# Zero matmuls in TensorE's waits, another order of the first four units, and four rounds of ones on ScalarE, in a one-core DLRM tower

## What is computed

```python
e = stack([tbl_f[ids[:, f]] for f in range(40)], axis=1)    # 512 x 40 x 32, 40 table lookups
i, j = triu_indices(40, k=1)                                # 780 pairs of fields
z = einsum('bpd,pde,bpe->bp', e[:, i], bilinear, e[:, j])   # one 32x32 matrix a pair
h = concatenate([z, dense_ctx], axis=1)                     # 512 x 796
h = maximum(h @ W_top1 + b_top1, 0)                         # 512 wide
h = maximum(h @ W_top2 + b_top2, 0)                         # 256 wide
y = h @ W_top3
```

## Time and profile before

| | us |
|---|---|
| median of 3 runs | 204.15 (202.26 to 205.39) |
| the profiled execution | 202.93 |
| its span, first to last instruction | 201.1 |
| TensorE busy in the span | 180.2 |
| VectorE busy in the span | 159.4 |
| ScalarE busy in the span | 50.9 |

### The profile page before, as it was taken

The page is one execution under the profiler, slowest core; times in us unless marked ns, Lnnn a source line. Parts: engine busy times, 40 slices in busy tenths (PEclk is TensorE's granted clock), DMA queues, the critical chain, the costliest instruction groups (busy, mean ns, idle before and its releaser), DMA issues.

```text
span 201.1 us, 3168 instructions
## 1 busy us (share of the span) xinstructions
PE 180.2 (90%) x1328; PEld 55.9 (28%) x1328; DVE 159.4 (79%) x158; ACT 50.9 (25%) x83; POOL 96.6 (48%) x101
## 2 busy tenths in 40 slices
PE   0097959949999999999999999999999999999992
PEld 0032212302432222322323222223232222223442
DVE  0779995999899999999999874996998989741500
ACT  2001095195000394010025413116204000031520
POOL 3877777887777777777777777400000000000000
PEclk9999988996999999999999999999999999999998
DMA  6999700000000581011001001000000000000000
GB/s 166 384 390 405 284 13 13 13 15 10 16 15 13 171 326 15 13 16 14 13 14 17 16 13 14 10 3 0 0 3 2 0 0 0 3 0 0 0 0 0
DMA packets 7662, 12.07 MB, mean 60 GB/s; under 512 B 2752, under 2 KB 5712, under 8 KB 7520
## 3 DMA queue, kind: packets, MB, share of 16 engines
q1 hardware_dynamic: 4288, 10.24, 13.9%
q0 software_dynamic: 3072, 1.58, 4.7%
q10 hardware_dynamic: 288, 0.05, 0.2%
HBM read 11.86 MB, written 0.00 MB: 59 GB/s over the span
## 4 chain that ended last, share of the span: by engine, by line
PE 80%; DVE 14%; DMA 3%; issue 1%; SPq 0%; ACT 0%; DVEq 0%
PE y_ps L469 30%; PE z_ps L491 24%; PE t_ps L450 10%; PE t_ps L438 8%; DVE hot L363 6%; PE y_ps L505 3%; DMA table<-hot_tables 3%; DVE low L375 3%; DVE rest L373 3%; DVE prod L404 2%; PE y_ps L422 2%; PE y_ps L499 2%; PE t_ps L514 1%; PE z_ps L484 0%; DVE xt L380 0%
## 5 line engine op out<-in xcount | busy, mean ns | idle before, releaser
L404 DVE TENSOR_TENSOR prod<-y_ps,xt 128x1024 f32<-128x1024 f32 x100 | 115.6, 1216 | 17.1 <-PE y_ps L469 9.1
L268 POOL DMA_INDIRECT x_rows<-rows,row x96 | 96.1, 1001 | 29.2 <-issue 28.9
L469 PE MATMUL y_ps<-xt,m_sb 32*128 32x512 f32 x400 | 67.5, 658 | 0.0
L491 PE MATMUL z_ps<-prod,sel 128*32 128x512 f32 x400 | 53.3, 604 | 0.0
L338 ACT ACTIVATE xt<-xt 128x512 f32<-128x512 f32 (+2 forms) x60 | 36.6, 625 | 17.3 <-DVE xt L380 15.9
L469 PEld LDWEIGHTS y_ps<-xt,m_sb 32*128 32x128 f32 x400 | 23.4, 187 | 39.6 <-issue 32.1
L438 PE MATMUL t_ps<-hot,table 128*32 128x512 bf16 x144 | 15.9, 431 | 17.4 <-DVE low L375 16.4
L363 DVE TENSOR_SCALAR hot<-hot_id,number 128x2048 bf16<-128x2048 int16 x36 | 25.7, 760 | 7.1 <-DMA hot_id<-hot_ids 5.8
L450 PE MATMUL t_ps<-z_t,table 128*128 128x512 f32 x40 | 21.4, 634 | 0.0
L491 PEld LDWEIGHTS z_ps<-prod,sel 128*32 128x32 f32 x400 | 7.9, 107 | 38.6 <-issue 31.0
L342 ACT ACTIVATE z_t<-z_ps 128x512 f32<-128x512 f32 x7 | 4.2, 597 | 54.0 <-PE z_ps L491 54.0
(11 more groups left out here) (21 smaller groups left out, 35.8 us busy)
## 6 DMA issues: line engine op xcount, KB each, us to landing
hot_id<-hot_ids SPq DMA_DIRECT2D x4, 512.0 KB, 7.0
table<-w SPq DMA_DIRECT2D x1, 1792.0 KB, 7.6
x_rows<-rows,row POOLq DMA_INDIRECT x96, 2.4
table<-hot_tables SPq DMA_DIRECT2D x2, 640.0 KB, 9.5
table<-hot_tables SPq DMA_DIRECT2D x2, 512.0 KB, 6.4
m_sb<-mats SPq DMA_DIRECT2D x2, 512.0 KB, 12.5
m_sb<-mats SPq DMA_DIRECT2D x2, 384.0 KB, 11.0
m_sb<-mats SPq DMA_DIRECT2D x1, 640.0 KB
```

What stands on the lines that cost most here:

```text
L268: pool.indirect_dma_start(out=x_rows[:, g, c, :], out_offset=None, in_=rows, in_offset=bass.IndirectOffsetOnAxis(ap=row[:, n:n + 1], axis= ...
L404: nc.vector.tensor_tensor(prod[:, k % PROD_UNITS, 2 * half:2 * half + 2, :], y_ps[:, 2 * slot:2 * slot + 2, :], partners[half], ALU.mult). ...
L469: last = nc.tensor.matmul(y_ps[:, 2 * slot + place % 2, :], m_sb[rows, k, :], xt[rows, u, :], start=True, stop=True)
L491: last = nc.tensor.matmul(z_ps[s * DIM:(s + 1) * DIM, :], window, prod[:, k % PROD_UNITS, place, :], start=first, stop=(k == last_unit(b)) ...
```

## The change

`UNIT[0:4]` becomes (2,0), (2,1), (0,0), (1,1). VectorE clears one piece of `prod` as its first instruction, and TensorE then multiplies these zeros 24 times (`WARM`). It also multiplies zeros in front of rounds 8 and 16 (`SPLIT_FILL`, 7 matmuls each), three times four behind unit 0 and once four behind unit 6 (`FILL`). The ones of rounds 5, 9, 14 and 20 (`BY_SCALAR`) are made by ScalarE in two activations, |id - row| and relu(1 - that), into blocks 1 to 6 of `z_t`, which are free then. The ring of four is shared by the 32 rounds that VectorE keeps. `AFTER` has new numbers: 26 rounds stand ahead of all units where 19 did, and 15 mixes where 7 did.

```diff
+UNIT[0:4] = UNIT[2:4] + UNIT[0:2]
+WARM = 24
+FILL = 4
+SPLIT_FILL = 7
+BY_SCALAR = {5: 0, 9: 0, 14: 8, 20: 16}
+ONES_RING = 3
 AFTER = {
-    "hot": [-1, -1, -1, -1, -1, -1, -1, -1, -1, -1, -1, -1, -1, -1, -1, -1, -1, -1, -1, 0, 1, 1, 1, 1, 1, 1, 2, 2, 2,
-        3, 3, 3, 3, 4, 5, 8],
-    "l1": [18, 24, 27, 28, 29, 29, 30, 30, 31, 33, 34, 34, 41, 42, 43, 45, 47, 48, 49, 49],
-    "turn": [0, 8, 18, 24, 32, 33],
-    "mix": [-1, -1, -1, -1, -1, -1, -1, 0, 0, 0, 0, 0, 1, 1, 1, 1, 2, 4, 4, 5, 6, 6, 7, 7, 9, 9, 10, 10, 11, 11, 11,
-        12, 13, 13, 13, 14, 17, 20, 24, 24, 25, 26, 27, 27, 27, 28, 29, 29, 35, 37, 38, 38, 39, 39, 40, 41, 43, 45,
-        49, 50],
+    "fill": [0, 0, 0, 6],
+    "hot": [-1, -1, -1, -1, -1, -1, -1, -1, -1, -1, -1, -1, -1, -1, -1, -1, -1, -1, -1, -1, -1, -1, -1, -1, -1, -1, 0,
+        1, 1, 4, 6, 6, 6, 6, 6, 7],
+    "l1": [18, 24, 26, 27, 28, 28, 31, 32, 33, 34, 36, 37, 41, 41, 43, 44, 46, 47, 48, 49],
+    "turn": [0, 8, 18, 24, 32, 38],
+    "mix": [-1, -1, -1, -1, -1, -1, -1, -1, -1, -1, -1, -1, -1, -1, -1, 0, 0, 1, 2, 2, 3, 3, 3, 5, 7, 7, 7, 9, 9, 11,
+        12, 13, 14, 14, 14, 14, 18, 20, 25, 25, 25, 26, 26, 26, 26, 28, 29, 32, 34, 34, 35, 35, 36, 36, 36, 37, 38,
+        42, 43, 45],
 }
@@ schedule()
-        for what in ("hot", "l1", "mix"):
+        for what in ("fill", "hot", "l1", "mix"):
@@ ones(j), new: where a round's ones lie
+            if j in BY_SCALAR:
+                n = 2 * (scalar_rounds.index(j) % ONES_RING)
+                return z_t[:, 1 + n:3 + n, :]...  # as bf16
+            return hot[:, vector_rounds.index(j) % HOT_RING, :, :]
@@ scalar
             act.dma_start(number[:], numbers).then_inc(number_in, 16)
+            act.dma_start(negative[:], negatives).then_inc(negative_in, 16)
             act.dma_start(sel[:], select).then_inc(sel_in, 16)
             for what, k in steps:
+                if what == "hot":
+                    for j in [j for j in scalar_rounds if BY_SCALAR[j] == k]:
+                        o, r = ROUND[j]
+                        n = scalar_rounds.index(j)
+                        act.wait_ge(hot_id_in[o], 16)
+                        act.wait_ge(negative_in, 16)
+                        if n >= ONES_RING:
+                            act.wait_ge(hot_used, scalar_rounds[n - ONES_RING] + 1)
+                        columns = ones(j).rearrange("p f b -> p (f b)")
+                        nc.scalar.activation(columns, hot_id[:, o, :], ACT.Abs,
+                                             bias=negative[:, n:n + 1]).then_inc(ones_half, 1)
+                        act.wait_ge(ones_half, n + 1)
+                        nc.scalar.activation(columns, columns, ACT.Relu, bias=negative[:, len(BY_SCALAR):],
+                                             scale=-1.0).then_inc(ones_done, 1)
@@ vector
+            nc.vector.memset(prod[:, 0, 0, :], 0.0).then_inc(cleared, 1)
             dve.wait_ge(number_in, 16)
...
-                    if k >= HOT_RING:
-                        dve.wait_ge(hot_used, k - HOT_RING + 1)
-                    nc.vector.tensor_scalar(hot[:, k % HOT_RING, :, :]...
+                    if k not in BY_SCALAR:
+                        n = vector_rounds.index(k)
+                        if n >= HOT_RING:
+                            dve.wait_ge(hot_used, vector_rounds[n - HOT_RING] + 1)
+                        nc.vector.tensor_scalar(ones(k)...
@@ tensor
+            def fill(count, start):
+                for _ in range(count):
+                    nc.tensor.matmul(z_ps[0:DIM, :], sel[:, 0:SEL_COLS].bitcast(BF16)[:, 0:DIM],
+                                     hot_id[:, 1, 0:BATCH].bitcast(BF16), start=start, stop=start,
+                                     skip_group_check=True)
+            pe.wait_ge(cleared, 1)
+            zeros = prod[:, 0, 0, :].bitcast(BF16)
+            for _ in range(WARM):
+                nc.tensor.matmul(y_ps[:, 0, :], zeros[:, BATCH:BATCH + P], zeros[:, 0:BATCH], start=True, stop=True)
             for what, k in steps:
+                if what == "fill":
+                    fill(FILL, AFTER["fill"][k] < LAG)
                 if what == "hot":
+                    if r == 0 and o == 1:
+                        pe.wait_ge(sel_in, 16)
+                        pe.wait_ge(hot_id_in[1], 16)
+                    if r == 0 and o > 0 and AFTER["hot"][k] < 0:
+                        fill(SPLIT_FILL, True)
...
-                    pe.wait_ge(hot_done, k + 1)
+                    if k in BY_SCALAR:
+                        pe.wait_ge(ones_done, scalar_rounds.index(k) + 1)
+                    else:
+                        pe.wait_ge(hot_done, vector_rounds.index(k) + 1)
...
-                    if u == t:
-                        x_there(pe, t)
+                    if all(w != u for _, w in UNIT[:k]):
+                        x_there(pe, u)
```

More of the change, by code:

```diff
@@ L136, in vector_schedule, with ones_count @@
     return steps
+def ones_count(k, by_scalar):
+    return len([j for j in range(k + 1) if (j in BY_SCALAR) == by_scalar])
 def picked(o):
@@ L148, in ends_bank, with bass_dlrm_tower @@
     return what == "hot" and k in [picked(o) for o in range(HOTS)]
-def bass_dlrm_tower(nc, ids, rows, hot_ids, numbers, hot_tables, dense, mats, w1, b1, w2, b2, w3, select, dense_sel, out):
+def bass_dlrm_tower(nc, ids, rows, hot_ids, numbers, negatives, hot_tables, dense, mats, w1, b1, w2, b2, w3, select, dense_sel, out):
     steps = schedule()
@@ L173, in x_there @@
             engine.wait_ge(turned, GATHER_POS.index(t) + 1)
+    vector_rounds = [j for j in range(len(ROUND)) if j not in BY_SCALAR]
+    scalar_rounds = [j for j in range(len(ROUND)) if j in BY_SCALAR]
     def mix_slot(g, s):
@@ L205, in bass_dlrm_tower @@
         number = sb("number", [P, HOTS, MAX_ROWS])
+        negative = sb("negative", [P, len(BY_SCALAR) + 1])
         hot = sb("hot", [P, HOT_RING, G, BATCH], BF16)
@@ L217, in bass_dlrm_tower, with ones @@
         w1_sb = weight_cols[:, 0:BLOCKS * N1].rearrange("p (b n) -> p b n", b=BLOCKS)
+        def ones(j):
+            if j in BY_SCALAR:
+                n = 2 * (scalar_rounds.index(j) % ONES_RING)
+                return z_t[:, 1 + n:3 + n, :].rearrange("p b c -> p (b c)").bitcast(BF16).rearrange(
+                    "p (f c) -> p f c", f=G)
+            return hot[:, vector_rounds.index(j) % HOT_RING, :, :]
         def upper(words):
@@ L226, in bass_dlrm_tower @@
         ids_in = sem("ids_in")
+        cleared = sem("cleared")
+        ones_half = sem("ones_half")
+        ones_done = sem("ones_done")
         row_done = sem("row_done")
         number_in = sem("number_in")
+        negative_in = sem("negative_in")
         hot_id_in = [sem(f"hot_id_in{o}") for o in range(HOTS)]
@@ L360, in _ @@
                         dve.wait_ge(hot_id_in[o], 16)
-                    if k >= HOT_RING:
-                        dve.wait_ge(hot_used, k - HOT_RING + 1)
-                    nc.vector.tensor_scalar(hot[:, k % HOT_RING, :, :].rearrange("p f b -> p (f b)"),
-                                            hot_id[:, o, :], number[:, o, r:r + 1], None,
-                                            ALU.is_equal).then_inc(hot_done, 1)
+                    if k not in BY_SCALAR:
+                        n = vector_rounds.index(k)
+                        if n >= HOT_RING:
+                            dve.wait_ge(hot_used, vector_rounds[n - HOT_RING] + 1)
+                        nc.vector.tensor_scalar(ones(k).rearrange("p f b -> p (f b)"), hot_id[:, o, :],
+                                                number[:, o, r:r + 1], None, ALU.is_equal).then_inc(hot_done, 1)
                     if r == 0:
@@ L387, in _ @@
                     t, u = UNIT[k]
-                    if u == 0 and t >= 2:
+                    if u != t and all(v == w or v != t for v, w in UNIT[:k]):
                         x_there(dve, t)
@@ L438, in _ @@
                             last = nc.tensor.matmul(t_ps[f * DIM:(f + 1) * DIM, :], pieces[piece][:, f, :],
-                                                    hot[:, k % HOT_RING, f, :], start=(r == 0 and piece == 0),
+                                                    ones(k)[:, f, :], start=(r == 0 and piece == 0),
                                                     stop=(r == n - 1 and piece == 2), skip_group_check=True)
@@ L565 @@
         numbers[:, o, :n] = np.arange(P * n).reshape(P, n)
+    negatives = np.ones((P, len(BY_SCALAR) + 1), np.float32)
+    for n, j in enumerate(sorted(BY_SCALAR)):
+        o, r = ROUND[j]
+        negatives[:, n] = -(np.arange(P) * HOT_ROWS[o] + r)
     hot_tables = np.zeros((P, HOTS, G, MAX_ROWS, DIM), np.float32)
@@ L577 @@
         "numbers": numbers,
+        "negatives": negatives,
         "hot_tables": hot_tables.reshape(P, HOTS, G, MAX_ROWS * DIM),
```

## The result

The changed kernel takes 193.74 us (median of 4 runs, 193.54 to 194.19) against 203.2 for the kernel before (201.77 to 205.39). The ratio is 0.956, 95% interval 0.948 to 0.964. The profiled execution of the changed kernel takes 193.84 us; its span is 192.0, 9.1 us less than before.

The account below looks back on a forecast made before the run. VectorE's queue, with 4.5 us idle, was taken to bound the head up to unit 8. Head -6.8 and steps +0.3 gave -6.5 us: 196.4 from 202.93, 197.7 from the median; 197.0 given, range 194.5 to 200.4.

Parts of the forecast that it names:

- the head: From 9.64 us until VectorE starts unit 8 at 65.91; forecast 6.8 us shorter, from 7.3 and 6.5.
- Rivals 2 and 3: Zeros don't count for the clock: 204.3 us, chance 0.06; Abs and Relu each need a table load: 205, 0.04.
- rivals 1 and 4: Clock falls once or twice: 198.7 to 200.4 us, chance 0.12; gain lost behind unit 8: 199, 0.06.
- everything behind it follows at a fixed distance: Behind VectorE's queue up to unit 8: what comes off that road comes off the end.
- small extra DMA: Load of the added input at the start, said to lie in VectorE's wait for the first ids until 5.76 us.
- My walk: VectorE's queue followed step by step from 9.64 us: table 3's pieces end at 34.0, unit 8 at 59.4 by pace.
- Busy time less the four comparisons: VectorE from 9.64 us to unit 8: 51.75 - 2.8 = 48.9 us, so unit 8 at 58.6.
- The first layer's steps: Steps placed between units behind unit 8: +0.4, -0.4, +0.2 and 0 to 0.6 more, taken as +0.3 us.
- the base: Time the gain is taken from: profiled execution 202.93 us gives 196.4, median 204.15 gives 197.7; 197.0 given.
- nine more rounds on VectorE: Walk's rounds after 24.0 us, said to reach 29.6 on VectorE with TensorE at 30.6.
- The first product's 2.4 us: Wait of 2.37 us before unit 0, put down to ScalarE's mixes; said to vanish with (2,0) first.
- the turns stand further ahead of their use: Transposes behind unit 8, with the mixes: ahead of their use by more than the 6.8 us they lose.

Follow-up runs that it names:

- a_noscalar: Changed kernel with all 36 rounds of ones on VectorE, none on ScalarE: 196.64 us.
- a_nowarm: Changed kernel without its 24 first zero matmuls, the 30 later ones kept: 196.01 us.
- b_again: Kernel before, run once more unchanged: 203.03 us, ratio 1.0003.
- b_warm: Kernel before plus the memset, the 24 first zero matmuls and the added input with its load; order and rounds as before: 201.13 us, ratio 0.993.
- t_tensor: Kernel before plus the small 128x5 input alone, loaded by nobody: 201.15 us, ratio 0.9924.
- t variants: Kernel before with small additions alone, such as an input, a load or a memset; usable times 201.2, 201.15 and 203.04 us.
- t_dup: Kernel before plus one more small load on ScalarE's queue from an existing input, no new tensor: 203.04 us, ratio 1.004.
- t_memset: Kernel before plus the memset and TensorE's wait for it; run under the disturbance, time not usable, wait for the output's transfer 2.5 us.
- e_notensor: Changed kernel without the added input, its numbers in free columns of `numbers`; disturbed, time not usable, wait for the output's transfer 2.5 us.
- a_nofill: Changed kernel with its 24 first zero matmuls but without the other 30: 194.03 us.
- a_order_only: Changed kernel without any zero matmul and with all rounds on VectorE; new order and added input stay: 198.82 us.
- b_scalar: Kernel before with rounds 5, 9, 14 and 20 on ScalarE and the added input; order as before, no zeros: 200.86 us, ratio 0.991.

## Why the prediction was right or wrong

**The bound was right.** VectorE's queue sets the head, and what leaves it reaches the end: the two later stages kept their length within 0.1 us. The comparisons cost 0.7 us each (a_noscalar), the 24 zeros hide in the wait for the first table and the first rounds are fast (a_nowarm), the later ones hide too. Rivals 2 and 3 (zeros don't count, ScalarE too slow by table loads) are refuted, rivals 1 and 4 didn't come about.

**The step that failed** is "everything behind it follows at a fixed distance". I took for granted that what comes off the road to unit 8 comes off the end and no more, and put the output's transfer at no change. Behind the last block the kernel took 15.73 us before and takes 14.24 now, because the added input goes with a transfer of the output that is waited for 1.1 us instead of 2.6. I had listed the input only as a "small extra DMA" that lies in a wait. These 1.5 us are the largest part of the miss: without them the time would have been some 195.2, inside my range. The wait of 2.6 us stood in the profile of before, but nothing in it said that an input would shorten it.

**A term was sized too small.** For the head I took 6.8 from two ways of adding up, 7.3 and 6.5; it was 7.7, and unit 8 came at 58.19 where I gave 58.6 to 59.5. My walk kept 0.9 us more than needed up to unit 0 (34.0 against 33.06), as it added durations where the next instruction starts before the last one's end: seven comparisons take 4.64 us from start to start and not 4.83, the pieces of tables 1 and 2 2.39 and 2.92 and not 2.46 and 2.98. Busy time less the four comparisons, 48.9 us, was the better way: 48.48. The first layer's steps cost 0.1 where I took 0.3. With all of it: -7.7 + 0.1 - 1.5 = -9.1 us, the difference of the spans.

My 197.0 also held 0.6 us for the base: it lies halfway between 196.4, from the profiled execution, and 197.7, from a median of 204.15 that a fourth run brought down to 203.2. So the miss of 3.3 us is 1.5 for the transfer, 0.9 for the head, 0.2 for the first layer's steps, 0.6 for the base and 0.1 of scatter. The lower end of my range doesn't follow from its own working: 202.93 - 7.3 is 195.6, not 194.5. And the walk's "nine more rounds on VectorE" are eight, as round 20 is ScalarE's; its 29.6 is reckoned with eight.

**Two readings were wrong and cost nothing.** The first product's 2.4 us were put down to ScalarE's mixes, as the row says. The six mixes that it needs were done by 29.2 us (12 in 7.59 us from 25.41), and unit 0's matmuls ran from 30.18 to 32.27 at half clock: TensorE was the one awaited, as the row of b_again has it. And I wrote that the turns stand further ahead of their use than what they lose, without looking at the last transpose. In the order before it stands in front of unit 33, at 131.0 us, about when the last gathers land: where it had to wait for them it started at 129.85 (b_warm), 131.22 (t_tensor) and 132.39 us (b_again). In profiles of the kernel before and its t variants the stretch from the second transpose to the last matmuls takes 131.0 us where it doesn't wait (three of five), 131.7 with a wait of 0.88 and 133.1 with one of 2.26. Without the move of that transpose to unit 38, a head shorter by 7.7 us would have met it, as an estimate from these starts; b_warm's profile gives back 1.2 of 2.6 us there. The move is part of the change that I had not priced.

**The parts, from the medians:** order and input together 3.9 us, of which the input is 1.4 (t_tensor: 1.2 to 1.5); zeros 1.05 to 2.2 and ScalarE's rounds 2.9 to 4.0, each more where the other is missing. In the order before, neither the first 24 zeros nor ScalarE's rounds are worth anything clear of noise.

## What to carry to other kernels

When one engine's queue is the bound, sum its busy time in that stretch and subtract what leaves: here that came nearer than walking it with paces (48.9 and 49.8 us against 48.65). Then look for the next fixed date behind it (here the last gathers), since a gain in front is only kept if the steps tied to that date move too. Try parts alone in the old kernel, and compare them with an old kernel that has the same inputs: ScalarE's rounds were worth nothing clear of noise there and 3 to 4 us in the new order, and the 1.6 us that the zeros seemed to bring there are, within noise, what the added input brings alone.

Where a kernel gets or loses an input or output tensor, compare the last transfer before explaining the rest of the difference.

## What the hardware showed that I had not expected

- The output of 2 KB takes 2.8 to 3.5 us from issue to landing in the five profiles without the added input (before, b_again, t_dup, t_memset, e_notensor), and 1.4 us in all fifteen kernels with one input of 2.5 KB more, loaded or not.
- Matmuls of zeros raise the granted clock: behind 24 of them the first real round takes 0.66 us, without them 1.3. The clock stood at 1.00 over a pause of 1.76 us (a_nofill) and fell behind one of 2.28 us (a_order_only), as it did behind 2.75 us in the earlier trace rows; but it also stood over 2.75 us (a_order_only) and 2.83 us (b_warm).
- The four runs of the changed kernel lie within 0.65 us, those of the kernel before within 3.6. That the first zeros do this isn't shown: a_nowarm has 2.5 us, but b_scalar and a_order_only, without zeros too, have 0.9.
